# Mamba scan kernel: rows of C 14 columns further, more products with B on GpSimd, another order on ScalarE

## The reference

```
rn = resid * rsqrt(mean(resid * resid, -1) + EPS) * norm_w
skip = rn @ skip_w.T
x_in = rn @ in_w.T
conv = conv_b + sum(xp[:, k:k + L, :] * conv_w[:, k] for k in range(K))   # xp: x_in, padded
x = silu(conv)
delta = softplus(x @ wd1.T @ wd2.T + wd2_b)
A = -exp(A_log)
Bm = x @ wB.T
Cm = x @ wC.T

def step(h, inp):                       # over the L positions of a sequence
    h = exp(d_l[:, :, None] * A) * h + (d_l * x_l)[:, :, None] * b_l[:, None, :]
    y_l = einsum('ben,bn->be', h, c_l)

y = ys + x * W_D
y = y * silu(skip)
return resid + y @ out_w.T
```

## Time and profile before

| | |
|---|---|
| median of 3 runs | 1789.19 us (1787.57 to 1790.89) |
| profiled execution, its own time | 1791.06 us |
| its span | 1789.3 us |
| PE busy | 1686.4 us (94%) |
| DVE busy | 1453.3 us (81%) |
| ACT busy | 1068.6 us (60%) |
| POOL busy | 1063.4 us (59%) |
| granted TensorE clock, mean | 0.982 |

### The profile page before, as it was taken

The page is one execution under the profiler, slowest core; times in us unless marked ns, Lnnn a source line. Parts: engine busy times, 40 slices in busy tenths (PEclk is TensorE's granted clock), DMA queues, the critical chain, the costliest instruction groups (busy, mean ns, idle before and its releaser), DMA issues. The chain is left out here.

```text
span 1789.3 us, 26479 instructions
## 1 busy us (share of the span) xinstructions
PE 1686.4 (94%) x9294; PEld 1330.9 (74%) x9294; DVE 1453.3 (81%) x2301; ACT 1068.6 (60%) x1872; POOL 1063.4 (59%) x668
## 2 busy tenths in 40 slices
PE   8989999899999999877999999999999999999999
PEld 3556666666766666566888888888899788888888
DVE  6899999999999999999877777775366876666665
ACT  7887887878887886878443444433444444344442
POOL 3899999999999998999722222221445322222220
PEclk9999999999999999989999999999999999999999
DMA  6323433343433334362011111121000021111111
GB/s 214 107 94 111 120 112 114 105 127 107 115 106 111 122 109 119 97 214 80 17 38 26 29 33 36 34 54 30 1 0 1 1 60 44 45 43 48 48 47 38
DMA packets 116542, 132.18 MB, mean 74 GB/s; under 512 B 19008, under 2 KB 65216, under 8 KB 116288
## 3 DMA queue, kind: packets, MB, share of 16 engines
q1 hardware_dynamic: 116416, 130.59, 25.4%
HBM read 102.22 MB, written 4.72 MB: 60 GB/s over the span
## 5 line engine op out<-in xcount | busy, mean ns | idle before, releaser
L396 POOL TENSOR_TENSOR m_U<-m_U,m_C 128x1024 f32<-128x1024 f32 x255 | 554.3, 2193 | 43.0 <-DVE m_U L967 43.0
L543 PEld LDWEIGHTS m_y<-ident,m_U 128*128 128x128 f32 x2048 | 248.5, 146 | 106.7 <-issue 72.6
L967 DVE TENSOR_TENSOR_SCAN m_U<-m_dA,m_carry,m_U 128x512 f32<-128x512 f32 x256 | 309.8, 1264 | 9.3 <-ACT m_dA L796 8.5
L967 DVE TENSOR_TENSOR_SCAN m_U<-m_dA,m_U 128x512 f32<-128x512 f32 x256 | 295.2, 1204 | 11.3 <-ACT m_dA L796 11.3
L543 PE MATMUL m_y<-ident,m_U 128*128 128x128 f32 x2048 | 280.0, 282 | 20.0 <-POOL m_U L396 19.5
L796 ACT ACTIVATE m_dA<-high,m_negA 128x512 f32<-128x512 f32 x256 | 170.9, 684 | 57.1 <-DVE m_U L967 56.6
L796 ACT ACTIVATE m_dA<-even,m_negA 128x512 f32<-128x512 f32 x256 | 169.5, 683 | 42.0 <-DVE m_U L967 40.2
L1266 POOL TENSOR_TENSOR SW<-g_Rt 128x512 f32<-128x512 f32 x32 | 39.7, 1271 | 256.8 <-DMA g_CT<-SW 237.1
L1266 POOL TENSOR_TENSOR SW<-f_Rt 128x512 f32<-128x512 f32 x32 | 41.0, 1309 | 213.4 <-DMA f_CT<-SW 213.4
L524 PE MATMUL m_psB<-m_stack,m_pick 128*128 128x512 f32 x169 | 86.1, 509 | 40.0 <-DVE m_U L950 38.1
L1455 ACT ACTIVATE g_sil<-g_psG 128x512 f32<-128x512 f32 x64 | 38.3, 599 | 126.9 <-PE g_psG L1325 126.9
(11 more groups left out here) (412 smaller groups left out, 4459.3 us busy)
## 6 DMA issues: line engine op xcount, KB each, us to landing
m_C<-bc_rows SPq DMA_DIRECT2D x256, 256.0 KB, 3.2
m_B<-bc_rows SPq DMA_DIRECT2D x87, 256.0 KB, 3.5
f_CT<-SW SPq DMA_DIRECT2D x128, 64.0 KB, 2.1
g_CT<-SW SPq DMA_DIRECT2D x128, 64.0 KB, 2.1
even<-in_ffn_w SPq DMA_DIRECT2D x16, 256.0 KB, 5.4
g_z_raw<-g_turned_z SPq DMA_DIRECT2D x112, 32.0 KB, 1.9
out<-res SPq DMA_DIRECT2D x7, 512.0 KB, 2.8
res<-in_x SPq DMA_DIRECT2D x1, 3072.0 KB, 12.6
```

Of the source, the lines that this page charges most:

```text
L396: pool.tensor_tensor(weighted[:, at, :, :], state[:, at, :, :], C[:, M % C_RING, :].unsqueeze(1).to_broadcast([P, PE_E, CHUNK]), ALU.mult) ...
L543: last = nc.tensor.matmul(y[:, t, j * P:(j + 1) * P], weighted[:, M % U_RING, j, t * P:(t + 1) * P], ident[:, :], start=False, stop=n == N ...
L967: nc.vector.tensor_tensor_scan(u, dA[:, s % A_RING, :], u, carry[:, e, n:n + 1] if q else 0.0, ALU.mult, ALU.add).then_inc(scan_done, 1)
```

## The change

The buffer of C gets 14 more columns at its start, and its 8 rows lie behind them. One table says for each of the 16 passes which units' product with B is GpSimd's: 5 and 5 in the first chunk, 7 and 7 in odd chunks, 7 and 5 in even ones, and 7 and 7 in the last. Before, it was 5 in the first pass and then 4, 7, 5, 6 by turns. On ScalarE, in the first chunk, `cv0` and `in1` move from slot 4 to slot 5, the first `double` from 5 to 6 and the second from 8 to 17, and `silu_g` gets a slot of its own, 15. In the last chunk one `sum` moves from slot 2 to 3 and one `square` from 3 to 6.

```diff
-    FIRST_POOL, AHEAD = (3, 7, 10, 12, 15), 3
-    ON_POOL = ((2, 4, 7, 9, 12, 14), (3, 7, 11, 14), (2, 4, 6, 9, 11, 13, 15), (2, 5, 8, 11, 14))
+    EVEN, ODD, AHEAD = ((1, 3, 5, 7, 9, 11, 13), (2, 5, 8, 11, 14)), ((1, 3, 5, 7, 9, 11, 13), (1, 3, 5, 8, 10, 12, 14)), 3
+    ON_POOL = ((3, 7, 9, 11, 13), (2, 5, 8, 11, 14)) + (ODD + EVEN) * (CHUNKS // 2 - 1) + ((1, 3, 5, 7, 9, 12, 14), (1, 3, 5, 8, 10, 12, 14))
...
-        C = sb("C", [P, C_RING, CHUNK])
+        C = sb("C", [P, C_RING * CHUNK + 14])[:, 14:].rearrange("p (r t) -> p r t", r=C_RING)
...
-                  "first": {3: (), 4: ("cv0", "in1")},
-                  "late": [(0, "sum", 8), (1, "square", 8), (2, "sum", 9), (3, "square", 9), (7, "norm", 8),
+                  "first": {2: (), 3: (), 4: (), 5: ("cv0", "in1"), 15: ("silu_g",)},
+                  "late": [(0, "sum", 8), (1, "square", 8), (3, "sum", 9), (6, "square", 9), (7, "norm", 8),
...
-        pool_units = [M for M in range(ALL_UNITS) if M % N in (ON_POOL[M // N % (2 * PASSES)] if M >= N else FIRST_POOL)]
+        pool_units = [M for M in range(ALL_UNITS) if M % N in ON_POOL[M // N]]
...
-                elif M in (5, 8):
-                    part("double", M // 8)
+                elif M in (6, 17):
+                    part("double", M // 17)
                 for name, k in parts_of(ACT_AT, M):
-                    if name[:4] == "silu" and (name, k) != ("silu_g", 0):
+                    if name[:4] == "silu":
                         (silu_x if name == "silu_x" else silu_gate)(k)
-                        if (name, k) == ("silu_x", 1):
-                            silu_gate(0)
                         nc.scalar.preload_act_table_set(EXP_LN_SET)
-                    elif name[:4] == "silu":
-                        continue
                     else:
                         part(name, k)
```

## The result

The changed kernel takes 1800.84 us (median of 5 runs, 1800.35 to 1801.30). The kernel before takes 1789.19 us beside it. The ratio is 1.006 with an interval of 1.0048 to 1.0071: slower by 0.6%. The forecast of 1767 us and its range are wrong; the first rival, at 1803 us, is what happened.

What follows compares the result with a forecast made beforehand. VectorE was taken as the bound, GpSimd close behind. Six middle chunks -15.3, first chunk -4.5 and last -3.6 sum to -23.4 us: 1767.7 from the profiled 1791.1, 1765.8 from the median, stated as 1767, range 1762 to 1774.

Steps and rivals of the forecast that it cites:

- the first rival: GpSimd's product with C (L396) stays at 2.19 us and GpSimd becomes the bound: 1803 us, chance 0.15.
- I take 2.00: GpSimd's product with C (L396): shifting C's rows 14 columns brings it from 2.19 to 2.00 us.
- a law of nearness: GpSimd's products: rows 0 or 4 to 15 columns apart modulo 512 carry the surplus, 2189 against 2001 ns.
- Rival 1: L396 unchanged: first chunk keeps about 3 us, three pairs +13, last pass loses 2; 1803 us, chance 0.15.
- The point at which GpSimd decides: Pair of chunks: slower GpSimd-bound outcome holds where L396 gains less than 0.07 us.
- the high end: Upper price of L396, L352's pattern twice, 2.36 us: a pair grows by another 12 us, to about 1840.
- The moved products: 15 products with B go from VectorE to GpSimd: 1.11 us each off VectorE, 1.95 us each on GpSimd.
- The pair, at the price assumed: Two whole chunks with L396 at 2.00 us: VectorE 194.5 us, GpSimd 193.6, lasting about 196.6 us.
- rival 3: Pairs of chunks: ScalarE's bursts become late, new waits of 1 to 2 us a pair; about 1772 us, chance 0.13.
- First chunk: ScalarE's new order saves 3.4 us of VectorE's stalls, one moved product 1.1: 4.5 us shorter.
- Last chunk: ScalarE's order saves 1.8 us, two moved products 2.2, less 0.4 charged for GpSimd: -3.6 us.
- The rule that spoke against the shift: The skill's 2.5-cycle floor for GpSimd's two-input operations: 2.13 us for 1024 elements at any address, so no gain worth having.

Runs made afterwards that it cites:

- K17: GpSimd alone, one layout of its two-input product: 512 columns, two dense inputs at a good d; 1088 ns.
- K16: GpSimd alone, one layout of its two-input product: 512 columns, all rows at one column; 1262 ns.
- E3: Kernel before with only the new table of GpSimd's products: 1804.65 us, ratio 1.0075.
- E4: Kernel before with only ScalarE's new order in the first and last chunk: 1786.04 us, ratio 0.9972.
- E8: Kernel before with C in rows of 514, 3 columns ahead, and ScalarE's new order, old table: 1786.59 us, ratio 0.9977.
- E6: Changed kernel with C 3 columns ahead instead of 14, in rows of 514: 1769.76 us, ratio 0.9887 to the kernel before.
- E1: Separate kernel, none of the reference: GpSimd alone multiplies in 20 layouts, six times each, VectorE still; two-block products took about 1995 to 2344 ns.
- E5: Separate kernel: GpSimd alone multiplies two rows of 512 columns at 36 pairs of starting columns; 1088 to 1092 or 1260 to 1263 ns.
- K1: GpSimd alone, layout of the product with C as in the kernel before; 2167 ns.
- K4 to K6: GpSimd alone, layouts of the product with C with the output's place varied; the first of them, written into another buffer, took the same as K1.
- K7: GpSimd alone, layout of the product with B; 1995 ns.
- K12: GpSimd alone, a layout compared with K7 for where the output lies, not written into the block read; own time not given.
- K13: GpSimd alone, a layout compared with K7 for where the output lies, written into the block read; own time not given.
- K15: GpSimd alone, K7 with its operands swapped; 2336 ns.

## Why the prediction was wrong

**The step that failed** is "I take 2.00, the row with the same number of elements, two dense reads and a distance outside 0 to 15". The price of L396 stayed at 2.19 us. Three rows had been read as a law of nearness. But L352 and L363 differ in d modulo 4 as well, 0 against 1 or 2, and L381 reads only one input densely: 512 columns with two dense inputs cost 1088 ns at a good d (K17), 50 more than its 1038, and a bad d adds another 174 (K16, 1262). The row that could have told it stood beside them, and I named it as what spoke against me: L396 doesn't change over d = 4 to 15. A product that always has one cheap and one dear block must be so even, and no shift by an even number can change that. The price was also at hand: half way between 2.00 us and 2.36, the prediction's own price for two blocks like L352's, is 2.18.

**What followed from it.** At 2.19 us the prediction gave a pair of 205.1 us of GpSimd's work and 206.1 us in time. Measured: 204.8 and 206.3. The profiled executions, cut at the first scan of a chunk (us; E3 has the table alone, E4 the order alone, E8 order and rows of 514, E6 all three):

| stretch | before | changed | E3 | E4 | E8 | E6 |
|---|---|---|---|---|---|---|
| first chunk | 111.6 | 107.5 | 110.0 | 108.0 | 108.1 | 107.1 |
| the six between | 605.9 | 618.9 | 619.2 | 605.9 | 605.7 | 594.8 |
| last chunk | 102.4 | 104.4 | 106.1 | 100.9 | 100.1 | 98.4 |
| blocks behind | 937.8 | 937.0 | 935.8 | 937.6 | 936.9 | 934.9 |

Rival 1 had -3, +13 and +2 us for the first three rows. Measured: -4.1, +13.0 and +1.9. So not only its number came, but its mechanism too.

The point at which GpSimd decides was put at 0.07 us less for each L396; the gain was 0.003. The chances were the second mistake: 0.15 for the only price that the trace showed for this form against 0.85 for prices that it did not show, and a range that left the first out. A slip beside it: at the high end a pair would grow by 64 x 0.17 = 10.9 us and not by 12.

**The moved products** were sized rightly on GpSimd: 15 of them, 15 x 1.95 = 29.3 us, and 29.7 us more busy time. On VectorE the page shows 11.6 us less and not 15 x 1.11 = 16.7. Part of it is how busy time adds up: an instruction that follows without a gap overlaps its forerunner by about 0.09 us (1.20 us long, 1.11 from start to start), one behind a wait counts in full, and there are some 50 waits more. E8 against E6 gives the time for 15 products and their waits: 16.8 us by the medians, where I had 15.3 in the pairs, 1.1 in the first chunk and 1.8 (2.2 less 0.4) in the last, 18.2. By the table above it is 10.9, 1.0 and 1.7 us, and some 2 in the blocks behind, which no edit touches. So the first and the last chunk were sized rightly, and the pairs gave less.

**The pair, at the price assumed.** I had 194.5 us of work and 2.1 us of waits, 196.6. E6 shows 195.0 and 3.1, 198.2. The waits for ScalarE are 1.9 us, as expected; 1.2 us are for GpSimd, which I had at nothing. The longer one, before unit 30 of the odd chunk, is in the pass in which seven products and four of delta x x (L352) come together:

```profile
430.88 2.46 DVE L963 TENSOR_TENSOR_SCAN m_U<-m_dA,m_carry,m_U 128x512 f32<-128x512 f32 x2 [0.91 <-POOL m_U L363]
```

So rival 3 gave the size but not the cause: ScalarE's bursts cost nothing new.

That E6's 1769.8 us still came within 3 us of the forecast is in part luck. Against the kernel before, the six chunks gave 11.1 us where I had 15.3; the blocks behind made up for it with 2.9, where I had nothing. Over the eight profiled executions of the whole kernel they take 934.9 to 938.8 us, and why they differ no run here shows.

**First chunk.** VectorE in order of time, changed kernel, with its idle time in brackets, to set beside the earlier trace rows:

```profile
50.95 4.56 DVE L963 TENSOR_TENSOR_SCAN m_U<-m_dA,m_U 128x512 f32<-128x512 f32 x4
56.63 1.22 DVE L946 TENSOR_TENSOR m_U<-even,m_psB 128x1024 f32<-128x1024 f32 x1 [1.11 <-PE m_psB L524]
57.77 2.33 DVE L963 TENSOR_TENSOR_SCAN m_U<-m_dA,m_U 128x512 f32<-128x512 f32 x2
62.31 2.34 DVE L963 TENSOR_TENSOR_SCAN m_U<-m_dA,m_U 128x512 f32<-128x512 f32 x2 [2.21 <-ACT m_dA L796]
...
84.50 2.34 DVE L963 TENSOR_TENSOR_SCAN m_U<-m_dA,m_U 128x512 f32<-128x512 f32 x2 [0.65 <-ACT m_dA L796]
...
91.85 2.34 DVE L963 TENSOR_TENSOR_SCAN m_U<-m_dA,m_U 128x512 f32<-128x512 f32 x2 [1.65 <-ACT m_dA L796]
```

The stall before unit 6 is gone (units 5 and 6 run as one group from 50.95 us). A stall of 2.21 us comes before unit 8, at 62.31 where I had 62.6; 0.65 us before unit 15, where I had 0.6; 1.65 us before unit 17, where I had 1.6. One was missed: 1.11 us before the product ahead of unit 7, for a spread of B that TensorE makes behind `cv0+` and `in1`. Behind it VectorE waits for ScalarE all the same, so it probably cost nothing; no run shows that by itself. The first chunk lasts 107.5 us instead of 111.6; -4.1 where I had -4.5.

**Last chunk.** E4 gives -1.5 us for the order, where I had -1.8. In the changed kernel the order still saves 1.7 (106.1 in E3, 104.4 here). It is the two moved products that turn from a gain into a loss: VectorE waits 3.8 us for GpSimd's products, where I had charged 0.4 for the cheap L396. In the first chunk the order saves 3.6 us on the old table and 2.5 on the new. Together that is 5.1 us and 4.2 in the profiled executions. By the medians it is 4.9 on the old table, and on the new one 2.0 or 3.8, as the changed kernel and E3 are each set against their own runs of before or against each other.

**The rule that spoke against the shift.** E1 has 1995 ns for 1024 elements, and in the same kernel 2338, from nothing but the starting columns. The Trainium skill, GPSIMD Engine Reference, section Instruction dispatch, has a floor of about 2.5 cycles per element with two inputs, an estimated 2.13 us for 1024 elements at its 1.2 GHz. The measured 1995 ns is below it, so it is no floor here. The consequence that I drew from it, no gain from this shift, came all the same, but by d and not by a floor.

DMA was free, as said: the loads of C take 4.3 us to land in the changed kernel in place of 3.2, but no wait of GpSimd in the Mamba block is for a DMA.

## What to carry to other kernels

Where two engines are within 1% of each other, moving work between them pays only if the receiving engine gets faster first, so measure that price by itself before betting on it; a kernel that runs one form in 20 layouts does it in one go. When a form's duration is even over many addresses, ask which property all of them share before concluding that a new address differs. And read a price that lies half way between two others as a possible mean of both, above all where an instruction has two blocks.

## What the runs showed of the hardware that was not expected

The time of GpSimd's product of two float32 inputs in SBUF depends on d, the second input's starting column less the first's, modulo 4, which is 16 bytes. 512 columns cost 1088 to 1093 ns where it is 1 or 2, and 1256 to 1263 ns where it is 0 or 3 (E5, 36 pairs). Where the output lies, in place or not, makes no difference (K1, K4 to K6; K7, K12, K13), nor does distance beyond that remainder. VectorE's work beside it adds 1% at most (2189 ns in the kernel before against 2167 alone). Other operations and types were not run. It isn't symmetric: with operands swapped d changes its sign, so 1 becomes 3, and L363's form goes from 1995 to 2336 ns (K7, K15). The Trainium skill, SBUF — State Buffer, section Door 1: The DMA port swizzle, speaks of lines of 16 bytes in SBUF whose crossing costs; the period measured here agrees with that length. Whether such lines are the cause, and why 1 and 2 are the cheap remainders, no run here shows.
